# Layer-norm tables centred by TensorE, weight means on ScalarE, fold matrices on GpSimd, and a new order of calls, in a one-core AdaLN transformer block with experts

## The reference, cut to what matters

```python
mod = (silu(c) @ wmod).reshape(16, 6, 1, 128)          # sa, ca, ga, sb, cb, gb
h = layernorm(x) * (1 + ca) + sa                        # 16 x 256 x 128
x0 = sqrt(128) * h + pos
for i in range(4):
    g = layernorm(x0, ln1_s[i], ln1_b[i])
    q, k, v = g @ Wq[i] + bq[i], g @ Wk[i] + bk[i], g @ Wv[i] + bv[i]
    x0 = x0 + linear_attention(q, k, v) @ Wo[i] + bo[i]
    g = layernorm(x0, ln2_s[i], ln2_b[i])
    x0 = x0 + relu(g @ W1[i] + b1[i]) @ W2[i] + b2[i]
x = x + ga * layernorm(x0, lnf_s, lnf_b)
h = layernorm(x) * (1 + cb) + sb
x = x + gb * (experts(h, top 2 of 8) + shared(h))
```

## Time and profile before

| | |
|---|---|
| Median of three runs | 619.46 us (618.18 to 620.15) |
| Profiled execution: its time | 617.45 us |
| Its span | 615.6 us |
| Granted clock, mean | 0.975 |
| TensorE busy (PE) | 576.7 us, 94% |
| VectorE busy (DVE) | 437.6 us, 71% |
| ScalarE busy (ACT) | 391.8 us, 64% |
| GpSimd busy (POOL) | 266.6 us, 43% |

### The profile page before, as it was taken

How to read it: one execution, slowest core, us unless ns; L and a number is a source line. 1 busy time by engine, 2 the same in 40 slices (tenths; PEclk the granted TensorE clock), 3 DMA queues, 4 the chain that set the end, 5 groups by cost and what they waited for, 6 DMA issues and landing times.

```text
span 615.6 us, 13067 instructions
## 1 busy us (share of the span) xinstructions
PE 576.7 (94%) x4562; PEld 540.8 (88%) x4562; DVE 437.6 (71%) x1433; ACT 391.8 (64%) x1378; POOL 266.6 (43%) x421
## 2 busy tenths in 40 slices
PE   4859999998999999998999999999999999999987
PEld 2439889998899999998899999998989999998876
DVE  4684576768886776768787676767787666667774
ACT  1654767696676666687676666588576666666551
POOL 5122366666314236656314246656324244446310
PEclk9678999999999999999999999999999999999998
DMA  9500051040000000000000000000000000000000
GB/s 275 170 4 1 2 194 43 1 172 1 2 18 19 2 1 2 2 1 2 2 18 19 2 1 2 2 1 2 2 19 18 1 2 2 1 2 1 2 18 18
DMA packets 10769, 16.04 MB, mean 26 GB/s; under 512 B 960, under 2 KB 8076, under 8 KB 10320
## 3 DMA queue, kind: packets, MB, share of 16 engines
q1 hardware_dynamic: 8208, 11.40, 5.8%
q0 software_dynamic: 880, 2.82, 1.6%
q10 hardware_dynamic: 1616, 0.98, 0.6%
HBM read 13.07 MB, written 2.14 MB: 25 GB/s over the span
## 4 chain that ended last, share of the span: by engine, by line
PE 83%; DVE 7%; ACT 6%; POOL 1%; issue 1%; DMA 1%; SPq 1%; DVEq 0%
PE psD L1533 20%; PE psB L1533 19%; PE psA L1533 18%; PE psC L1533 18%; PE psB L1590 1%; PE psD L1590 1%; PE psC L1590 1%; PE psA L1590 1%; DMA M<-in_attn_b 1%; PE psC L1639 1%; PE psB L1639 1%; PE psA L1639 1%; POOL guB L808 0%; ACT H L454 0%; POOL ziB L802 0%
## 5 line engine op out<-in xcount | busy, mean ns | idle before, releaser
L780 POOL TENSOR_TENSOR rstdD<-msD,neghalf 128x2 f32<-128x2 f32 x36 | 25.5, 710 | 71.5 <-ACT ziD L429 55.4
L780 POOL TENSOR_TENSOR rstdA<-msA,neghalf 128x2 f32<-128x2 f32 x36 | 25.7, 713 | 70.0 <-ACT eqkA L429 60.7
L780 POOL TENSOR_TENSOR rstdC<-msC,neghalf 128x2 f32<-128x2 f32 x36 | 25.6, 711 | 36.5 <-ACT eqkC L429 35.7
L780 POOL TENSOR_TENSOR rstdB<-msB,neghalf 128x2 f32<-128x2 f32 x36 | 25.0, 695 | 31.6 <-ACT eqkB L429 30.2
L1533 PE MATMUL psD<-w,H 128*128 128x128 f32 x256 | 31.5, 276 | 0.1
L1533 PE MATMUL psB<-w,H 128*128 128x128 f32 x256 | 31.3, 275 | 0.0
L1533 PE MATMUL psC<-w,H 128*128 128x128 f32 x256 | 31.2, 275 | 0.0
L1533 PE MATMUL psA<-w,H 128*128 128x128 f32 x256 | 31.2, 275 | 0.0
L1533 PEld LDWEIGHTS psD<-w,H 128*128 128x128 f32 x256 | 29.8, 192 | 0.3 <-ACT H L454 0.3
L1533 PEld LDWEIGHTS psA<-w,H 128*128 128x128 f32 x256 | 30.0, 192 | 0.0
L1533 PEld LDWEIGHTS psC<-w,H 128*128 128x128 f32 x256 | 30.0, 192 | 0.0
(11 more groups left out here) (556 smaller groups left out, 2422.9 us busy)
## 6 DMA issues: line engine op xcount, KB each, us to landing
M<-modulation_rows SPq DMA_DIRECT2D x2, 1280.0 KB, 8.5
M<-modulation_rows SPq DMA_DIRECT2D x1, 2560.0 KB, 8.7
out<-X SPq DMA_DIRECT2D x16, 128.0 KB, 1.9
w<-in_attn_W POOLq DMA_DIRECT2D x1, 1024.0 KB, 9.8
M<-in_attn_W SPq DMA_DIRECT2D x3, 256.0 KB, 5.9
X<-in_attn_x_in ACTq DMA_DIRECT2D x1, 512.0 KB, 4.3
wo<-in_attn_Wo POOLq DMA_DIRECT2D x1, 256.0 KB, 5.8
M<-in_attn_W ACTq DMA_DIRECT2D x1, 256.0 KB, 5.5
```

The costliest lines, as they stand in the source:

```text
L780: pool.tensor_tensor(b.rstd[:, :], b.ms[:, :], neghalf[:, :], ALU.pow).then_inc(b.s_rstd.sem, 1)
```

## The change

1. Loads. The parameter table `par` gets bo and b2 as 8 more rows, and a 128 x 128 matrix `cen` (the identity less 1/128) is loaded from the constants, all on SyncE's queue ahead of the position table and the biases. The two broadcast loads of bo and b2 go. x's first load is cut in two, by pairs of chains. GpSimd issues the loads of Wo and W2 only when the second of these has landed.
2. bo and b2 are centred and spread over the partitions by TensorE: four products each of a broadcast column of `parT` with `cen`, which ScalarE copies out (`bias_rows(k)` on both).
3. Wo's rows are centred by ScalarE, one layer a call (`less_wo_means(l)`), layer 0 ahead of the loop, 1 to 3 in its first step. `less_means` goes.
4. Fold matrices 2 to 7 are made by GpSimd; 0 and 1 stay on VectorE.
5. VectorE's modulation part 1 is cut into parts 1 to 4, spread over the start. Its scratch moves out of chain D's hidden buffer, so the wait of D's first relu for it goes.
6. The order of calls is new on all four engines, ahead of the loop and in it. Outputs are the same.

```diff
-            for n, a in enumerate((ln1_s, ln1_b, ln2_s, ln2_b)):
+            for n, a in enumerate((ln1_s, ln1_b, ln2_s, ln2_b, bo, b2)):
                 sync.dma_start(par[n * LAYERS:(n + 1) * LAYERS, :], a).then_inc(s_par, 16)
-            sync.dma_start(K[:, C_FIRST:], consts[:, C_FIRST:]).then_inc(s_pos, 16)
+            sync.dma_start(cen, consts[:, C_CEN:]).then_inc(s_par, 16)
+            sync.dma_start(K[:, C_FIRST:C_CEN], consts[:, C_FIRST:C_CEN]).then_inc(s_pos, 16)
...
+            def bias_rows(k):                                   # ScalarE
+                act.wait_ge(s_parps, k + 3)
+                act.activation((bo_all, b2_all)[k][:, :, :], A.ps[:, 1, :].rearrange("p (l n) -> p l n", n=D), ACT.Copy)\
+                    .then_inc(s_condT, 1)
+            def less_wo_means(l):                               # ScalarE
+                if l == 0:
+                    act.wait_ge(s_wo, 16)
+                act.activation(wo[:, l, :], wo[:, l, :], ACT.Copy, scale=-1.0 / D,
+                               accum_out=wosum[:, l:l + 1]).then_inc(s_lesswo, 1)
+                act.wait_ge(s_lesswo, 2 * l + 1)
+                act.activation(wo[:, l, :], wo[:, l, :], ACT.Identity, scale=-float(D),
+                               bias=wosum[:, l:l + 1]).then_inc(s_lesswo, 1)
...
+            def fold_matrix(n):                                 # GpSimd, n = 2 to 7
+                l, k = n // 2, n % 2
+                if n == 2:
+                    pool.wait_ge(s_parT, 1)
+                    pool.wait_ge(s_fold, 2)
+                sc = parT[:, 2 * k * LAYERS + l:2 * k * LAYERS + l + 1]
+                sh = parT[:, (2 * k + 1) * LAYERS + l:(2 * k + 1) * LAYERS + l + 1]
+                pool.tensor_scalar(fold[:, n, 0:P - 1], base[:, 0:P - 1], sc, None, ALU.mult)
+                pool.tensor_copy(fold[:, n, P - 1:P], sh).then_inc(s_fold, 1)
...
+            pool.wait_ge(s_xfirst[1], 16)                       # ahead of the loads of Wo and W2
...
+            def bias_rows(k):                                   # TensorE
+                if k == 0:
+                    pe.wait_ge(s_parT, 1)
+                else:
+                    pe.wait_ge(s_condT, k + 2)
+                for l in range(LAYERS):
+                    n = (4 + k) * LAYERS + l
+                    last = mm(A.ps[:, 1, l * D:(l + 1) * D], parT[:, n:n + 1].to_broadcast([P, P]), cen)
+                last.then_inc(s_parps, 1)
```

In the loop most edits swap neighbours. Two examples, from TensorE's and ScalarE's lists:

```diff
                 out_project2(D_, i, 3)
+                transposes(C, i, 7)
                 logits(A, i)
-                transposes(C, i, 7)
...
                 squares(D_, i, 8)
+                relu(C, i, 3, 0)
                 tokensT(A, i)
                 transposed(D_, i, 7)
                 tokensT(B, i)
                 relu(D_, i, 3, 0)
                 relu(D_, i, 3, 1)
-                relu(C, i, 3, 0)
```

More of the change, by code:

```diff
@@ L534, in _ @@
                 transposed(C, i, 1)
-                key_exps(A, i, 1)
-                squares(D_, i, 2)
                 if i == 0:
                     high(5)
+                squares(D_, i, 2)
+                key_exps(A, i, 1)
                 query_exps(A, i, 1)
+                relu(C, i, 0, 0)
                 transposed(B, i, 2)
-                relu(C, i, 0, 0)
+                transposed(D_, i, 1)
                 relu(C, i, 0, 1)
-                transposed(D_, i, 1)
                 key_exps(B, i, 1)
-                query_exps(B, i, 1)
                 if i == 0:
@@ L569, in _ @@
                 query_exps(D_, i, 1)
+                transposed(B, i, 3)
+                squares(A, i, 5)
                 att_transposed(C, i, 1)
-                squares(A, i, 5)
                 relu(B, i, 1, 0)
@@ L598, in _ @@
                 transposed(C, i, 4)
+                transposed(A, i, 5)
                 squares(D_, i, 5)
-                transposed(A, i, 5)
+                squares(B, i, 6)
                 key_exps(C, i, 2)
                 query_exps(C, i, 2)
-                squares(B, i, 6)
                 transposed(D_, i, 4)
@@ L1233, in _ @@
             in_scale(B, 0)
+            bias_plus_one(0, 1)
             in_enter(B, 0)
+            fold_matrix(1)
+            bias_plus_one(1, LAYERS)
+            modulation(0)
             first_rows(C)
-            low(0)
-            low(1)
-            modulation(0)
-            scale(A, 0, 1)
-            first_rows(D_)
-            in_scale(C, 0)
+            first_rows(D_)
+            scale(A, 0, 1)
+            in_scale(C, 0)
+            in_scale(D_, 0)
+            in_enter(D_, 0)
@@ L1253, in _ @@
             positive_queries(B, 0, 0)
             masked(B, 0, 0)
-            divided(A, 0, 0)
+            low(1)
+            scale(D_, 0, 1)
             divided(B, 0, 0)
-            fold_matrix(2)
-            scale(D_, 0, 1)
-            in_enter(C, 0)
-            fold_matrix(3)
-            less_means(1)
+            modulation(3)
             low(2)
+            move(A, 0, 1)
             move(B, 0, 1)
+            modulation(4)
+            scale(C, 0, 1)
+            scale(B, 0, 2)
@@ L1295, in _ @@
                 low_part(A, i, 2)
+                move(D_, i, 1)
                 low_part(C, i, 1)
-                move(D_, i, 1)
                 scale(B, i, 3)
+                positive_keys(A, i, 1)
                 if i == 0:
                     low(5)
-                positive_keys(A, i, 1)
+                scale(D_, i, 2)
                 positive_queries(A, i, 1)
@@ L1333, in _ @@
                 masked(C, i, 1)
+                scale(B, i, 4)
+                positive_keys(D_, i, 1)
                 if i + 1 < STEPS:
                     in_stats(C, i + 1)
+                divided(C, i, 1)
                 low_part(B, i, 3)
-                positive_keys(D_, i, 1)
-                divided(C, i, 1)
+                move(A, i, 4)
                 positive_queries(D_, i, 1)
-                move(A, i, 4)
                 masked(D_, i, 1)
@@ L1512, in _ @@
                 if i + 1 < STEPS:
-                    move(B, i + 1, 1)
+                    move(A, i + 1, 1)
                 gate_up(C, i, 2)
                 if i + 1 < STEPS:
-                    move(A, i + 1, 1)
+                    move(B, i + 1, 1)
+                    scale(B, i + 1, 2)
                 finish(D_, i, 0)
```

429 lines of the change are left out of this document (212 added, 217 removed).

## The result

| | before | after |
|---|---|---|
| Median | 618.97 us (618.18 to 620.15, four runs) | 608.89 us (608.39 to 609.50, four runs) |
| Span of the profiled execution | 615.6 us | 607.1 us |
| Granted clock, mean | 0.975 | 0.997 |
| First transposes of A | 21.85 | 19.38 |
| A's first move | 38.53 | 32.12 |

The ratio is 0.9835, 95% interval 0.9818 to 0.9853, and the medians are 10.1 us apart, where 6.5 were forecast and 613.0 us as the time. The last four rows are landmarks of the profiles, in us from the start of the span. (The first expand starts at 50.24 in the timeline of the kernel before; the 50.44 of the prediction is where the chain of the earlier trace rows picks it up.) The kernel before was profiled in one of its faster executions, 617.45 us, so that the two spans are 8.5 us apart and the medians 10.1. The table says where the 8.5 come from.

What follows compares the result with a forecast made beforehand. TensorE was taken to bound the loop's step, so an earlier first expand moves the end. Gains 0.65 + 1.6 + 4.2 = 6.5 us from 619.46 gave 613.0 us; range 604.5 to 617.6, centre case 609.5 to 616 at 0.48.

Steps and rivals of the forecast that it cites:

- rival (1): Start and loop: clock holding 2.4 GHz adds 4.4 us, loop 4, gain up to 15; centre 608, below 609.5; chance 0.21.
- First transposes: Start of kernel to chain A's first transposes at 21.85: gain 0.65 us, from -1.4 to +2.2.
- clock held: Lower bound for the first transposes, 19.5 us, if TensorE, busy without a break from 8.9, keeps its clock.
- the choice of 21.2 between 19.5 and 23.3: Start taken for the first transposes, between clock held and clock down; the clock had fallen at 37 without long idle before.
- no slack: Ahead of the folds: modulation(0)'s 256 KB load lands near 15.1 us, against centring products and first rows ending at 15.0.
- From there to A's move: First transposes to both moves: 0.59 and 3.64 us gone, 2.6 put in (modulation(2) and (3) 1.9, low(1) 0.7); gain 1.6.
- From there to the first expand: Moves to the loop's first expand: b2's mean, most modulation and four fold matrices gone, 0.5 returned; gain 4.2 us.
- W2's mean on ScalarE: Ahead of the loop: eight activations of 0.33 us between transposed D and C, under D's keys and queries; included in 4.2.
- GpSimd's matrices: Six fold matrices on GpSimd, 0.5 us a pair, 3.0 in all, before stages where it idles: cost 0, bound 1.
- Rival (3): VectorE blocked by GpSimd for 0.5 us at each of six fold-matrix pairs: 3 us less gain, 616; chance 0.04.
- The loop: New order mostly swaps of neighbours, Wo's layers on ScalarE cost 0: net 0, bound 1 us a step either way.
- Rival (5): Last third of a step: relu of C ahead of A's tokens idles TensorE 0.60 to 2.6 us; 623; chance 0.10.

Runs made afterwards that it cites:

- before_fill: The kernel before with four more unused 256-column TensorE products in TensorE's wait ahead of the first fold: 614.95 us, ratio 0.9937.
- early_loads: The changed kernel with the loads of Wo and W2 issued at the start of GpSimd's program again: 611.03 us, ratio 0.9864.
- modulation_late: The changed kernel with modulation (2) and (3), six VectorE instructions, behind the moves again: 610.28 us, ratio 0.9845.
- fold_on_vector_2: The changed kernel with fold matrices 2 to 7 on VectorE again, rerun for an ordinary profile: 613.28 us, ratio 0.9902.
- old_loop_later: The changed kernel with the old order of calls in steps 1 to 3 alone, on all four engines: 605.60 us, ratio 0.9787.
- before_new_loop: The kernel before with only the loop's calls in the change's order, on all four engines: 621.57 us, ratio 1.0035.
- bias_broadcast: The changed kernel with bias tables by two broadcast loads (issued earlier than before), means on VectorE, no centring products: 616.21 us, ratio 0.9945.

## Why the prediction came out as it did

The direction was right and the time inside the range; the forecast gain was 3.6 us short. For the start rival (1) has the mechanism: 6.5 and 4.4 for the clock is 10.9, and the first expand moved 11.0. That the two agree to 0.1 us is luck. By its terms the three points below gain 2.9, 1.6 and 6.4 us, and 2.5, 3.9 and 4.6 were measured. That rival also had the loop give 4, and the loop took 2.5.

- *First transposes, forecast 0.65 of gain, measured 2.5.* The bound "clock held", 19.5, came true (19.38; it is a gain of 2.35, where the prediction's range says 2.2). The failing step was the choice of 21.2 between 19.5 and 23.3: I set the fall at 37 against TensorE's being busy, instead of asking what the kernel before would do with its wait of 2.3 us filled. before_fill shows that. Within it two errors cancel. TensorE was free at 12.84, not 15.0: 1.0 of the 2.2 us is the table, ready at 7.90 and not at 8.9, since the early loads land sooner (early_loads), and the rest is that I had priced all products ahead of the folds at half pace, where the second four centring products took 1.05 us for the 1.87 of the first. Then it stood 1.78 us for the modulation load, which I had put at "no slack".
- *From there to A's move, 1.6, measured 3.9.* The terms were mis-sized twice. Six modulation instructions cost 0.56 and not 1.9 (modulation_late), for most lie in VectorE's waits; and from 21.85 to 26.8 TensorE had run at 1.2 GHz.
- *From there to the first expand, 4.2, measured 4.6.* Right in sum. Of that, 1.3 is D's and C's keys and queries at full pace (2.73 us for 3.99), which was not in it, so the work taken off VectorE gave 3.4 of the 4.2.
- *W2's mean on ScalarE* hides but for 0.4 us: the copy of C's transposes stands behind it on ScalarE and ends at 37.76, so TensorE's next product starts 0.2 us late, at 37.81, and C's nine products, whose low part comes later still, take 1.40 us for the 1.15 of D's.
- *GpSimd's matrices*: 0.75 us a pair and not 0.5, and no wait for them shows. Rival (3) had the mechanism and the wrong instructions. Two of VectorE's were held up, 0.61 to 1.09 us and 0.42 to 0.80, both beside a bias addition of GpSimd and none beside a matrix. The first lies on the path. Of VectorE's, GpSimd's and TensorE's timelines:

```profile
21.89 1.09 DVE L1076 SCALAR_TENSOR_TENSOR xC<-ziC,in_rstdC,xC 128x128 f32<-128x128 f32 x2
...
22.05 0.78 POOL L831 TENSOR_TENSOR xB<-xB,bo_all 128x256 f32<-128x256 f32 x1 [2.82 <-DVE xnB L1093]
...
23.36 0.76 PE L1558 MATMUL psA<-vA,kpA 128*128 128x144 f32 x4 [0.54 <-DVE kpA L1116]
```

  VectorE's `kpA` starts behind it, at 22.90, though its last input was there at 22.40, and TensorE waits for `kpA`: up to 0.5 us. The same clash cuts the other way: on VectorE the matrices would have cost 3.4 us (fold_on_vector_2).
- *The loop, 0 with a bound of 1 us a step.* It lost 0.4 to 1.0 us between C's first moves of one step and the next (old_loop_later, before_new_loop). Rival (5) had the direction and the wrong place and mechanism: not a relu, but the density of TensorE's stream and one clash of VectorE and GpSimd. Reasoning about single swaps found neither.
- *The sum of the undone parts* (7.3, 4.4, 2.6, 2.1, 1.4 us) is 17.8, and 15.6 by the ratios, far above the gain of 10: most bring the clock down again, so each is charged for the same microseconds, and bias_broadcast, the largest, isn't a part undone as it was.

## What to carry to other kernels

Ahead of a dense loop, price a wait of TensorE at more than its length: it can halve the pace of the products behind it, and useless products in the wait may pay (3.0 to 3.9 us here for four). Read the pace off distances between starts, not off the clock's column alone. Judge a new order of calls by the distance between landmarks of one step and the next, with the rest held still: busy shares and listed waits showed nothing of the 1 us a step. When a part is undone to price it, put its loads back where they were. And a short VectorE instruction between SBUF tiles next to a row of GpSimd's additions can take as long as theirs.

## What was not expected of the hardware

- An instruction of VectorE between SBUF tiles beside GpSimd's additions took 0.69 to 0.71 us for 0.27, while one that reads PSUM kept 0.42, and so did one between SBUF tiles beside GpSimd's fold matrix (0.41).
- Of the same two instructions of these engines, 0.36 us apart, now one and now the other was held up, step by step, in one execution.
- 1.3 MB of loads, asked for 3.6 to 4.1 us earlier on another queue, delayed a 64 KB load by 4.5 us and left the first load of constants where it was.
- The same fold at the same moment of two executions took 0.81 us and 1.55, with the clock's column at 1.00 in the slower one too.
